# Two half-step feed-forwards around a selective scan, 16 chunks on one core: other orders of work in the first and in the last chunk

## The reference, cut to what matters

```
x = x + 0.5 * ffn(layernorm(x))      # x: (4, 2048, 512) float32
x = x + mamba(layernorm(x))
x = x + 0.5 * ffn(layernorm(x))
ffn(x):   xr, xk = mixes of x and of x one token earlier
          sigmoid(xr W_r) * (relu(xk W_k)^2 W_v)
mamba(x): xn = layernorm(x); xs, z = xn W_in           # 1024 channels each
          xc = silu(causal conv of 4 taps over xs)
          dt, B, C = xc W_x; delta = softplus(dt W_dt + b)
          h_t = exp(delta A) h_(t-1) + delta B xc      # 16 states a channel
          y = (sum_n C h + D xc) * silu(z);  return y W_out + x
```

## Time and profile before

| | |
|---|---|
| median of 3 runs | 4810.01 us (4800.88 to 4814.4) |
| profiled execution, its own time | 4806.88 us |
| its span in the trace | 4805.1 us |
| granted PE clock, mean | 0.958 of full speed |
| busy share of PE, DVE, ACT, POOL | 88%, 89%, 64%, 71% |
| DMA | 810.72 MB, 53.0% of 16 engines' span |

### The profile page before, as it was taken

The page is one execution under the profiler, slowest core; times in us unless marked ns, Lnnn a source line. Parts: engine busy times, 40 slices in busy tenths (PEclk is TensorE's granted clock), DMA queues, the critical chain, the costliest instruction groups (busy, mean ns, idle before and its releaser), DMA issues.

```text
span 4805.1 us, 58035 instructions
## 1 busy us (share of the span) xinstructions
PE 4236.8 (88%) x16672; PEld 2383.7 (50%) x16672; DVE 4291.5 (89%) x3394; ACT 3068.6 (64%) x6611; POOL 3430.0 (71%) x3584
## 2 busy tenths in 40 slices
PE   5777999998999899999998999899899989999787
PEld 2444555555555555545454555555555455554443
DVE  1799998989999899998989999899998999999991
ACT  3656666766667676666667666676666767666562
POOL 2666777777676877777677777877768687777771
PEclk9988999999999999999999999999999999999798
DMA  2445555565555555555565555555555555555551
GB/s 74 138 143 174 180 171 178 171 190 172 184 181 163 190 159 183 172 186 178 159 195 171 181 183 163 186 173 184 168 184 178 173 180 163 184 180 162 168 166 60
DMA packets 423055, 810.72 MB, mean 169 GB/s; under 512 B 41264, under 2 KB 41264, under 8 KB 418640
## 3 DMA queue, kind: packets, MB, share of 16 engines
q1 hardware_dynamic: 422736, 807.00, 53.0%
HBM read 772.25 MB, written 34.60 MB: 168 GB/s over the span
## 4 chain that ended last, share of the span: by engine, by line
PE 50%; DVE 21%; issue 10%; POOL 7%; ACT 7%; DMA 4%; SPq 0%; DVEq 0%; POOLq 0%; ACTq 0%
PE y_acc L572 10%; DVE decay L1099 10%; PE mm L601 9%; PE mm L488 8%; PE mm L477 8%; DVE g L1107 6%; POOL dbx L1304 5%; PE mm L514 4%; DMA c_all<-bc_scratch 4%; PE mm L499 3%; DVE xc L1045 3%; PE mm L536 2%; PE mm L524 2%; PE mm L548 1%; POOL xout L1293 1%
## 5 line engine op out<-in xcount | busy, mean ns | idle before, releaser
L1304 POOL TENSOR_TENSOR dbx<-u,b_all 128x1024 f32<-128x1024 f32 x1024 | 2414.7, 2358 | 427.8 <-DVE g L1107 399.3
L1099 DVE TENSOR_TENSOR_SCAN decay<-decay,state,dbx 128x1024 f32<-128x1024 f32 x1024 | 2406.1, 2350 | 176.0 <-ACT decay L907 160.5
L572 PE MATMUL y_acc<-ident,g 128*128 128x128 f32 x8192 | 1115.6, 283 | 262.6 <-DVE g L1107 258.8
L572 PEld LDWEIGHTS y_acc<-ident,g 128*128 128x128 f32 x8192 | 967.9, 145 | 718.0 <-DVE g L1107 424.0
L1107 DVE TENSOR_TENSOR g<-decay,c_all 128x1024 f32<-128x1024 f32 x1024 | 1244.8, 1216 | 38.3 <-PE y_acc L572 9.5
L904 ACT ACTIVATE decay<-delta,neg_a 128x512 f32<-128x512 f32 x1024 | 708.5, 692 | 36.8
L907 ACT ACTIVATE decay<-delta,neg_a 128x511 f32<-128x511 f32 x1024 | 686.8, 671 | 0.0
L913 ACT ACTIVATE state<-decay 128x2 f32<-128x2 f32 x1024 | 166.7, 163 | 743.5 <-DVE g L1107 742.8
L499 PE MATMUL mm<-wbuf_c,col 128*128 128x512 f32 x1024 | 461.9, 595 | 9.1 <-ACT delta L855 7.0
L1045 DVE SCALAR_TENSOR_TENSOR xc<-mm,conv_sb,xc 128x509 f32<-128x509 f32 (+2 forms) x384 | 285.7, 744 | 57.1 <-ACT xs_last L822 46.5
L499 PEld LDWEIGHTS mm<-wbuf_c,col 128*128 128x128 f32 x1024 | 184.9, 190 | 201.9 <-issue 196.4
(11 more groups left out here) (105 smaller groups left out, 5226.5 us busy)
## 6 DMA issues: line engine op xcount, KB each, us to landing
b_all<-bc_scratch SPq DMA_DIRECT2D x1024, 256.0 KB, 3.8
c_all<-bc_scratch SPq DMA_DIRECT2D x1024, 256.0 KB, 4.1
wbuf_d<-in_w_r SPq DMA_DIRECT2D x32, 1024.0 KB, 7.3
wbuf_c<-in_w_v SPq DMA_DIRECT2D x32, 1024.0 KB, 7.4
xin<-in_x SPq DMA_DIRECT2D x16, 1024.0 KB, 6.9
wbuf_c<-in_w_k SPq DMA_DIRECT2D x16, 1024.0 KB, 6.8
wbuf_d<-in_w_in SPq DMA_DIRECT2D x16, 1024.0 KB, 7.5
res_scratch<-rows SPq DMA_DIRECT2D x16, 1024.0 KB, 4.6
```

What stands on the lines that cost most here:

```text
L572: last = pe.matmul(y_acc[:, tb, j * P:(j + 1) * P], g[:, s % PAIRS, j, tb * P:(tb + 1) * P], ident[:, :], start=n == 0 and j == 0 and tb % ...
L1099: dve.tensor_tensor_scan(d, d, flat(dbx[:, s % DBX, :, :]), state[:, batch, s, 0:1], ALU.mult, ALU.add).then_inc(scan_done, 1)
L1304: pool.tensor_tensor(dbx[:, s % DBX, :, :], u[:, q % 2, :, :], b_all[:, s % BRING, :].unsqueeze(1).broadcast_to([P, QT, W]), ALU.mult).the ...
```

## The change

Five edits, all at the two ends. (1) The load of chunk 0 is SP's first transfer, ahead of the nine small ones. (2) In iteration -1 the products go round six banks, the two of `mm` and the four of `decay`, in place of two. (3) In iteration 15 the gate projections move from steps 27, 29, 32, 37, 58, 59, 60, 62 to 15, 16, 21 to 25, 27, with their evictions and weights (the second half of the gate weights comes into buffer d at step 15); the output projection of chunk 14 moves from steps 4/5, 19/20, 21/22, 23 to 4/5, 7/8, 10/11, 13/14 and its additions to 6, 9, 12, 15; the third pair of y's transposes moves from 61, 62 to 50, 51. (4) The output projection of chunk 15 begins at steps 59 to 62 of iteration 15, on the channel groups that are ready; the rest follows in iteration 16 directly behind the last `sum_g`, in four banks, the halves that need the last two channel groups last. (5) The last chunk is stored in four pieces of 128 tokens, each as soon as POOL has finished it.

```diff
--- before.py
+++ after.py
@@ -191,6 +191,17 @@
+        LAST = NCH - 1
+        Z_LAST = (15, 16, 21, 22, 23, 24, 25, 27)
+        GATE_LAST = (16, 17, 22, 23, 24, 25, 26, 28)
+        OUT_LAST, ADD_LAST = ((4, 5), (7, 8), (10, 11), (13, 14)), (6, 9, 12, 15)
+        TURN_LAST, GATE_Y_LAST = (50, 51), (51, 52)
+        PART_LAST = ((0, 0, 59), (0, 1, 60), (1, 0, 61), (1, 1, 62))
+        def moved(steps, last, it):
+            return last if it == LAST else steps
@@ -260,27 +271,37 @@
         OFFSET = {q[0]: q[1] for q in GROUPS}
+        EARLY = {f"z{e}": Z_LAST[e] for e in range(ET)} | {f"YT{4 + j}": TURN_LAST[j] for j in range(2)}
+        EARLY |= {f"o{n}": OUT_LAST[n][0] for n in range(TB)}
+        FILLED_LAST = [(EARLY.get(q[1], q[0]), *q[1:]) for q in FILLED]
+        GROUPS_LAST = [(name, off - p // 64, marks, emptied, b)
+                       for p, name, off, marks, emptied, b in sorted(FILLED_LAST, key=lambda w: w[0] % 64)]
         NUMBER = {q[0]: n for n, q in enumerate(GROUPS)}
+        NUMBER_LAST = {q[0]: n for n, q in enumerate(GROUPS_LAST)}
...
-        TURNS = {-1: {f"xs{e}": e % 2 for e in range(ET)},
-                 NCH: {f"f1{q}{n}": n % 2 for q in "Tkr" for n in range(CT)}}
+        FIRST = [q[0] for q in GROUPS if 0 <= q[1] - 1 < 1 or q[0] in ("dt0_0", "dt0_1")]
+        TURNS = {-1: {name: n % 6 for n, name in enumerate(FIRST)},
+                 LAST: {f"z{e}": e % 2 for e in range(ET)} | {"YT4": 0, "YT5": 1},
+                 NCH: {f"f1{q}{n}": n % 2 for q in "Tkr" for n in range(CT)} | {"YT6": 3, "YT7": 4, "o0": 0, "o1": 1,
+                                                                                "o2": 2, "o3": 5}}
...
         def bank(it, group):
-            return mm[:, home(it, group), :]
+            h = home(it, group)
+            return mm[:, h, :] if h < 2 else decay[:, (h - 2) // 2, (h - 2) % 2, :]
...
-            n, mine = NUMBER[group], home(it, group)
+            n, mine = moved(NUMBER, NUMBER_LAST, it)[group], home(it, group)
...
                     n, it = len(GROUPS) - 1, it - 1
-                name, off, marks, emptied, _ = GROUPS[n]
+                name, off, marks, emptied, _ = moved(GROUPS, GROUPS_LAST, it)[n]
@@ -310,6 +331,7 @@
+            sp.dma_start(xin[:, :, :], tokens_of(x, 0, 0)).then_inc(x_loaded, 16)
@@ -365,7 +387,7 @@
                         load_b(f, s + 6 - NSTEP)
-                    if back and s == LOAD["wo1"]:
+                    if back and it <= LAST and s == LOAD["wo1"]:
@@ -381,7 +403,7 @@
                         sp.dma_start(wbuf["d"][:, :, :], piece(w_in, 0, 0)).then_inc(wxs_loaded[0], 16)
-                    if scn and s == LOAD["wz0"]:
+                    if scn and s == moved(LOAD["wz0"], LOAD["wv0"], it):
@@ -403,6 +425,8 @@
                             after(mark(m_pe, f, "xs3"))
+                        elif it == LAST:
+                            after(mark(z_pe, it, "7"))
@@ -412,15 +436,22 @@
                         sp.dma_start(wbuf["a"][:, :, :], piece(w_out, 0, 0)).then_inc(wo_loaded[0], 16)
-                    if scn and s == LOAD["wz1"]:
+                    if scn and it < LAST and s == LOAD["wz1"]:
...
                         sp.dma_start(wbuf["b"][:, :, :], piece(w_in, 0, E + 512)).then_inc(wz_loaded[1], 16)
+                    if it == LAST and s == LOAD["wxs0"]:
+                        after(mark(m_pe, it, "xs3"))
+                        after(mark(f_pe[1], b - 1, "r3"))
+                        sp.dma_start(wbuf["d"][:, :, :], piece(w_in, 0, E + 512)).then_inc(wz_loaded[1], 16)
+                    if it == LAST and s == LOAD["wz1"]:
+                        after(mark(f_pe[1], b, "k3"))
+                        sp.dma_start(wbuf["b"][:, :, :], piece(w_out, 512, 0)).then_inc(wo_loaded[1], 16)
...
                                      xdbl[R:XR, :]).then_inc(bc_stored, 16)
-                    if ahead and s == LOAD["x"]:
+                    if ahead and it != -2 and s == LOAD["x"]:
@@ -440,12 +471,17 @@
                         sp.dma_start(wbuf["c"][:, :, :], piece(w_k, 0, 0)).then_inc(wk_loaded[0], 16)
-                    if back and s == LOAD["out"]:
+                    if back and it < NCH and s == LOAD["out"]:
...
                         sp.dma_start(tokens_of(out, b, (bt - 1) % BATCHES), xout[:, :, :]).then_inc(out_stored, 16)
+                    if back and it == NCH and s == LOAD["out"]:
+                        for tb in range(TB):
+                            after(mark(f_pool[1], b, f"o{tb}"))
+                            sp.dma_start(tokens_of(out, b, (bt - 1) % BATCHES)[:, tb, :],
+                                         xout[:, tb, :]).then_inc(out_stored, 16)
             run(body, sp)
-            sp.wait_ge(out_stored, 16 * NCH)
+            sp.wait_ge(out_stored, 16 * (NCH - 1 + TB))
@@ -519,7 +555,7 @@
                     pe.wait_ge(*free)
-                win = wbuf["cb"[e // 4]]
+                win = wbuf["cb"[e // 4] if k < LAST or e < 4 else "d"]
@@ -590,17 +626,21 @@
-            def out_proj(it, k, tb, part):
-                if part == 0:
-                    pe.wait_ge(y_dve.sem, y_dve.at(k, "g7"))
-                    if free := bank_free(it, f"o{tb}"):
+            def out_proj(it, k, tb, part, es=range(4)):
+                if part == 0 and 0 in es:
+                    pe.wait_ge(y_dve.sem, y_dve.at(k, "g7" if k < LAST else "g3"))
+                    if k == LAST and tb > 1:
+                        pe.wait_ge(saved, NSTEP * k + NSTEP - 1 + tb // 3)
+                    elif free := bank_free(it, f"o{tb}"):
                         pe.wait_ge(*free)
+                if k == LAST and part == 1:
+                    pe.wait_ge(y_dve.sem, y_dve.at(k, f"g{4 + max(es)}"))
...
                 wo = wbuf["ab"[part]]
-                for e in range(4):
-                    last = pe.matmul(bank(it, f"o{tb}"), gate[:, 4 * part + e, tb * P:(tb + 1) * P], wo[:, e, :],
+                for e in es:
+                    last = pe.matmul(bank(k + 1, f"o{tb}"), gate[:, 4 * part + e, tb * P:(tb + 1) * P], wo[:, e, :],
                                      start=part == 0 and e == 0, stop=part == 1 and e == 3)
-                if part == 1:
+                if part == 1 and 3 in es:
@@ -609,18 +649,33 @@
                     if s == 0:
+                        if it == NCH:
+                            out_proj(it, b, 2, 0, range(3))
...
                             sum_g(b, NSTEP - 1)
+                        if it == NCH:
+                            out_proj(it, b, 2, 0, (3,))
+                            turn_y(it, b, 6)
+                            turn_y(it, b, 7)
+                            out_proj(it, b, 2, 1, range(2))
+                            out_proj(it, b, 3, 0)
+                            out_proj(it, b, 3, 1, range(2))
+                            for n in range(TB):
+                                out_proj(it, b, n, 1, range(2, 4))
...
                         sum_g(it, s - 1)
+                    if it == LAST:
+                        for tb, part, p in PART_LAST:
+                            if p == s:
+                                out_proj(it + 1, it, tb, part, range(4 - 2 * part))
...
                     if scn:
-                        for e in at(YTURN, s):
+                        for e in at(moved(YTURN, (*YTURN[:4], *TURN_LAST, *YTURN[6:]), it), s):
                             turn_y(it, it, e)
-                    if back:
+                    if back and it < NCH:
@@ -632,9 +687,9 @@
                             sum_skip(it, q)
-                    if back:
+                    if back and it < NCH:
                         for n in range(TB):
-                            for part in at(OUT[n], s):
+                            for part in at(moved(OUT, OUT_LAST, it)[n], s):
@@ -646,7 +701,7 @@
                     if scn:
-                        for e in at(Z, s):
+                        for e in at(moved(Z, Z_LAST, it), s):
@@ -955,10 +1010,10 @@
                     if scn:
-                        for e in at(GATE_TANH, s):
+                        for e in at(moved(GATE_TANH, GATE_LAST, it), s):
...
                     if back:
-                        for e in at(GATE_TANH, s + 64):
+                        for e in at(moved(GATE_TANH, (), b), s + 64):
@@ -1120,13 +1175,13 @@
                     if scn:
-                        for e in at(GATE_SILU, s):
+                        for e in at(moved(GATE_SILU, GATE_LAST, it), s):
...
                     if back:
-                        for e in at(GATE_SILU, s + 64):
+                        for e in at(moved(GATE_SILU, (), b), s + 64):
...
                     if scn:
-                        for e in at(GATE_Y, s):
+                        for e in at(moved(GATE_Y, (*GATE_Y[:4], *GATE_Y_LAST, *GATE_Y[6:]), it), s):
@@ -1137,7 +1192,7 @@
                             ffn_gate(1, b, n)
-                        for n in at(OUT_ADD, s):
```

(1 more changed line is left out.)

## The result

The changed kernel takes 4777.57 us (median of 6 runs, 4771.43 to 4781.71), the kernel before 4809.66 beside it: ratio 0.9933 (95% interval 0.992 to 0.9946), or 32.1 us less where 34.8 were forecast. The profiled executions, on which the sum was made, differ by 35.5: 4806.88 and 4771.43, spans 4805.1 and 4769.6. The second is the fastest of its six runs.

| piece of the span | before | after | difference | forecast |
|---|---|---|---|---|
| to DVE's first statistics | 13.97 | 8.37 | -5.6 | -5.4 |
| from there to the first scan | 143.26 | 134.61 | -8.65 | -6.1 |
| first scan to the first g of chunk 15 | 4290.57 | 4288.56 | -2.0 | 0 |
| chunk 15, first to last g | 250.07 | 249.37 | -0.7 | -5.5 |
| last g to the last out addition | 34.42 | 18.49 | -15.9 | -15.9 |

The account below looks back on a forecast made before the run. At the ends it saw the start waiting for chunk 0's load, then PE with two banks, and a serial output projection last. 5.4 + 6.1 + 5.5 + 15.9 + 1.9 = 34.8 us off gave 4772.1, forecast as 4775, range 4763 to 4787.

Parts of the forecast that it names:

- Load first: Start: chunk 0's load issues at 0.74 instead of 6.86, statistics start at 8.55 instead of 13.97, saving 5.4 us.
- the bound of 3.9: Start: saving of only 3.9 us if the small loads stand behind x's megabyte and land at 10.
- Six banks: Front, iteration -1: PE no longer stops for banks; 0.8 + 3.1 + 2.2 = 6.1 us saved.
- Work moved inside chunk 15: Chunk 15: 4.7 + 2.9 + 4.4 us back, 6.5 added, net 5.5 us saved; range 0 to 9.
- the named signs of being wrong: Profile: statistics after 10, first scan under 8 us earlier, R matmuls 0.85, steps 9 to 28 over 4.6, last store 4 us.
- Nothing waits: Chunk 15: after checking moved waits such as k3 at step 52, claimed that none of them delays anything.
- the unknown clock: Chunk 15: less PE work in steps 29 to 40 may slow R matmuls, costing 0 to 7.0 us; taken as 0.
- Behind the last step: Tail: 32 matmuls instead of 64 after the last sum_g, ending at 4716.4 instead of 4732.29, saving 15.9 us.
- Four stores: End: the last quarter lands in 2.25 us where 1 MB took 4.2, saving 1.9 us.
- shorter only on PE: Rival: ACT, DVE and small loads hold the front (8.3 us), chunk 15 gives 0; 26 us, 4784; chance 0.17.
- Given back: Rival: last 32 matmuls wait or run slow, 13.9 less; 12 us in all, 4798, within 0.3%; chance 0.05.
- The low clock stays: Rival: thinned PE work keeps 160 matmuls slow, 70 us lost against 35 gained, 4845; chance of slower 0.04.

Follow-up runs that it names:

- the pair of single edits: Kernel before with only chunk 0's load first: 4803.22 us; kernel before with only the six banks of iteration -1: 4804.43 us.
- equal fronts: Seven traces, the changed kernel's and six variants', with its front unchanged; first scan at 141.44 to 146.16 us.
- the two kernels with the old banks: The kernel before, and the kernel before with only chunk 0's load as first transfer (4803.22 us).
- the later silus: Changed kernel with the first two gate evictions at steps 17 and 18, not 16 and 17: steps 16 to 18 took 11.47 us, chunk 15 249.18.
- The zeros: Changed kernel with two idle products on zeros in each of 14 light steps (18 to 40) of chunk 15: 4767.6 us, chunk 15 245.69.
- six traces: Traces with the work of these steps and no zeros in them; step 43 took 5.61 to 7.18 us.
- the single edit: Changed kernel with the last chunk stored in one piece: POOL's last end to span's end 4.72 us against 2.46, span 4775.2.
- both, timed: Changed kernel with the first two gate evictions one step later and idle zero products in light steps of iteration 15: 4765.6 us, ratio 0.9906.

## Why the prediction was right, and where not

The range held the result and the sum came within 2.7 us of it, but two of its five terms were off, the banks by 2.6 us too low and chunk 15 by 4.8 too high. That they offset each other is luck.

- **Load first**: 5.4 forecast, 5.6 measured. The small loads decide, as said; the bound of 3.9 did not come true. The first of them lands later than before behind the megabyte, 4.7 us after its issue in place of 1.6, but the last took 3.0 in place of 3.3.
- **Six banks**: 6.1 forecast, 8.65 measured. By its parts: four transposes 0.8 against 1.2; four stops 3.1, which by the pair of single edits are 4.1, for a stop costs 1.0 and not its bracket alone (between the two profiled executions 3.8, K being slower after); the taps 0.7 against 0.8; the rest of that part 1.5 against 2.9, of which 1.9 are the faster 32 matmuls. Those 1.9 are where the clock's changes fell, shown by equal fronts that differ by 4.7 us. The transposes and the stops, 1.4 too low together, are no chance: on the mean of the seven equal fronts the way from the statistics to the first scan is 8.3 us shorter than in the kernel before. The 0.8 that is left of the difference is less than the 1.0 by which the two kernels with the old banks differ there (143.26 and 144.27), and stays open.
- **Work moved inside chunk 15**: 5.5 forecast, 0.7 measured. This is the step that failed, in two places, and one of the named signs of being wrong came with it: steps 16 and 22 took 5.18 and 5.13, over the 4.6. "Nothing waits" overlooked that the product of step 15 needs the bank which the addition moved into that step empties: 1.5 us, shown by the later silus. And of the unknown clock I took the value 0, "since the same R came after low-load steps before". It cost some 3.2 (steps 22, 31, 43), inside the stated 0 to 7.0, of which the 1.3 of step 43 were absent from two of six traces; the first eight R matmuls took 0.72 each, not 0.85. The zeros gave all of it back and more. The reason given was a weak one: R did follow light steps before too, but thinning more of them made it slower. What was right is the piece taken out of step 23: 8.19 became 4.91, and a silu of 0.6 has come in, so 3.9 us went where 4.2 were forecast; with zeros ahead it is 4.57, the forecast value.
- **Behind the last step**: 15.9 forecast, 15.93 measured, at the pace of 0.43 that was assumed. (From the end of the last g to the last addition the forecast names 33.3 before; its own rows give 33.2.)
- **Four stores**: 1.9 forecast, 2.3 measured between the traces and again by the single edit. POOL finishes the pieces 3.4 us apart, and they landed 2.0 us after their issue (median), the single 1 MB store 4.2, so only the last piece is waited for. The Trainium skill's rule of at least 1 MiB a transfer (DMA: Bandwidth & Descriptors, Bandwidth) is one for bandwidth, and is not borne out at this place, where what counts is how soon the last piece lands.
- **The middle**, forecast at nothing, gave 2.0 us in the profiled pair. It is not a gain: from the first g of chunk 0 to that of chunk 15 the same instructions took 4284.6 to 4294.9 us over the kernels whose middle is untouched, 4285.5 after and 4287.6 before.

Of what the profile would show, xproj's end came at 133.5 where 136.5 was forecast; the signs for the first scan (14.25 us earlier), the statistics, steps 59 to 63 and the last store came as said.

Of the rivals, "shorter only on PE" had the R products at the low clock in chunk 15 right, but in the front all its bounds were too low. "Given back" did not come: the last 32 matmuls ran at pace. "The low clock stays" named the right danger with the wrong extent. The Trainium skill says that throttled is the default and activity releases it (TensorE: Matmul & The Clock Gate, Part 1), and the traces agree: 0.66 granted at 4590 to 4606, behind light steps, and 1.00 at 4663 to 4683, in dense work. But the slow matmuls were the first after light steps, not 160 in a row.

## What to carry to other kernels

Work taken off a busy engine's step leaves a light step behind, and the next dense group pays for it: look at the granted clock of the stretch before a group is thinned out, and put filler where PE idles ahead of work that others wait for. When an eviction is moved, list what frees each bank in its new step. And where equal instructions scatter by 5 to 10 us in a span of 4800, judge an edit by its own stretch of the trace, and time several runs before the whole is believed. Filler has its price too: in "both, timed" six matmuls on zeros (2.7 us) stood ahead of a `sum_g` that ACT waited 1.50 us for, and step 35 took 4.82, no better than the 4.50 to 4.99 of the traces without zeros.

## What was not expected

That more idle products make a kernel faster that already has one in each chunk: 152 matmuls on zeros and one shifted pair of silus brought 26 us (4777.57 to 4751.55), nearly as much as the 32 of the whole change, and with zeros in steps 1 and 2 of every chunk the runs also lie closer, 4751.49 to 4753.93 against 4771.43 to 4781.71. And that a stop of 0.78 us for a bank costs 1.0. Left open: which of the three places in the chunks that still vary most (steps 23, 41 and 54, by 1.1 to 1.7 us) would gain from filler as well; it was not tried. Nor was it tried whether less filler would do.
